# Sorted experts: the expert numbers of a chunk read behind the first product of its last tile, and their table written in two copies

## The chip, the cores and the metric

The program runs on one core of a Trainium2 chip. The metric is the device time of one execution in microseconds (us), as the median over several runs; lower is better. A core has five engines that run side by side, each with its own instruction queue: TensorE (PE, with its weight loads listed as PEld), VectorE (DVE), ScalarE (ACT), GpSimd (POOL) and SyncE (SP, which issues DMAs). Each queue is fed by a sequencer, a small processor that also executes the instructions for registers, branches and some of the waits on semaphores. In the profile the sequencer of TensorE stands as PEldq.

## The reference, cut to what matters

The network has two layers, each with an attention branch and a gated mixture-of-experts branch. The last part of the second layer is the one that this case is about:

```python
xs = x * scores
order = jnp.argsort(topk_ids)
sorted_x = xs[order]
g = _grouped_mm(sorted_x, routed_gate_w, tokens_per_expert)
u = _grouped_mm(sorted_x, routed_up_w, tokens_per_expert)
d = _grouped_mm(jax.nn.silu(g) * u, routed_down_w, tokens_per_expert)
routed_out = d[inv]
...
x = x + s * g
```

There are 8192 tokens of 128 numbers, 32 experts with a hidden size of 256, and each token goes to one expert. `s` is the attention branch, and the last `g` is the silu of shared plus routed output.

## The kernel before, in words

The kernel works in stages with a barrier between them. Stage 3 computes the second layer's attention and the choice of expert, and scatters each token's row (its scaled input, the attention result, the shared result and the residual) into a sorted buffer `srt` in HBM. The buffer has 96 tiles of 128 rows; all rows of a tile belong to one expert. At the end of stage 3 TensorE transposes the count that tells each tile's expert into one PSUM row, and VectorE's `table_rows` writes it as integers into `TE`: row j of `TE` holds eight numbers, the experts of the four tiles of chunk j-1 and then those of the four tiles of chunk j. It does so in three passes over 32 tiles each, through a small integer tile (L1846 to L1856).

Stage 4 (L1970 to L2200) works through the sorted tiles in 24 chunks of four. All of the routed weights lie in SBUF (`WE1`, `big` in the profile), and a product picks its expert's columns by a register. For a tile t the steps are:

- SP loads the chunk's rows (L2005) and, later, its tails with the other branches' values (L2008).
- PE transposes the rows (L2041), ACT copies the result to SBUF (L2100).
- PE makes the first product, gate and up in one, 512 columns wide (`up`, L2036). Here the weights' columns move past the array, and they are addressed by the expert's register.
- ACT applies silu (L2110), DVE multiplies by the up half (L2132).
- PE transposes the hidden rows (L2046), DVE copies them to SBUF (`turned`, L2136).
- PE makes the second product (`down`, L2055), again addressed by the expert's register.
- Once a chunk: DVE adds the tails (L2142), ACT applies the silu (L2104), DVE weighs and finishes (L2147, L2154, L2155), and POOL scatters the four tiles to the output with four indirect DMAs (L2194) behind a small instruction (L2191) that waits for L2155.

On TensorE the tiles are skewed by hand. An iteration for tile t issues `up(t)`, the row transpose of tile t+2, the hidden transposes of tile t-2 and `down(t-3)`, in this order. Before the four iterations of a chunk the function `experts(j)` reads row j of `TE`, eight registers at once; it is the `TENSOR_LOAD` on L2061. The second half of the eight serves the four `up` of this chunk, the first half serves the three `down` of the chunk ahead that are still due, and for its last iteration the chunk uses the same register list for its own tile.

The first two chunks and the last two are written out, and the twenty between them are a loop of ten rounds with two chunks in each (`pe.Fori`, its branch stands on L2087 in the profile). Inside the loop the semaphore values that are waited for are computed from the loop's counter, so a wait is made of a register instruction (`ALU_OP` or `FUSED_REGOPS`) ahead of the instruction that waits.

Of the kernel before, what the change touches and what calls it, by code (L numbers as in the profile page):

```python
# [25 lines left out]
ALU = mybir.AluOpType  # L26
# [3 lines left out]
P = 128  # L30
C = 128
# [12 lines left out]
E1, F1 = 32, 256  # L44
# [4 lines left out]
SORTED_TILES = NT + E1  # L49
IN_FLIGHT = 4  # L50
# [19 lines left out]
def mixed_layers(nc, x, w0, cols, rows, rot, cst, ws, wsd, we0, wd0, w1, we1, out):  # L70
# [10 lines left out]
    with ctx:  # L81
# [19 lines left out]
        WE1 = big[:, :].rearrange("p (e f) -> p e f", e=E1)  # L101
# [61 lines left out]
        ident = CST[:, C_ID:C_ID + P]  # L163
# [48 lines left out]
        pb = [ps[:, n, :] for n in range(8)]  # L212
# [4 lines left out]
        hT = early([P, 2, FC, S])  # L217
# [331 lines left out]
        part = early([E0, CAP, 4])  # L549
# [651 lines left out]
        TE = sb("TE", [1, SORTED_TILES // IN_FLIGHT + 1, 2 * IN_FLIGHT], I32)  # L1201
# [3 lines left out]
        def stage3():  # L1205
# [28 lines left out]
            end_of, new, dg, base, pages = (late([P, E1]) for _ in range(5))  # L1234
            need = sb("mx_need", [P, E1])
            cnt = sb("mx_cnt", [P, HALF])
            ci = [sb(f"mx_ci{m}", [P, E1], I32) for m in range(2)]
# [13 lines left out]
            xT = [attT, ROT[:, :].rearrange("p (g s) -> p g s", g=2)]  # L1251
            zA = [b.rearrange("p g t c -> p (g t) c") for b in (z, att)]
            n_w = E1 * 768 // HALF
            at = [E1 * 768 - 4 * PT * C]
# [15 lines left out]
            pb = [ps[:, n, :] for n in range(8)]  # L1270
# [35 lines left out]
            with nc.Block() as block:  # L1306
# [384 lines left out]
                def _(dve):  # L1691
# [150 lines left out]

                    def table_rows():

                        dve.wait_ge(s["table"], 1)
                        rows = ci[0][0:1, 0:E1].rearrange("p (j k) -> p j k", k=IN_FLIGHT)  # L1846
                        by_chunk = pb[0][0:1, 0:SORTED_TILES].rearrange("p (n j k) -> p n j k", k=IN_FLIGHT, n=SORTED_TILES // E1)
                        for n in range(SORTED_TILES // E1):
                            dve.drain()
                            dve.tensor_copy(rows, by_chunk[:, n, :, :])  # L1850
                            dve.drain()
                            for at, part in ((0, slice(IN_FLIGHT, 2 * IN_FLIGHT)), (1, slice(0, IN_FLIGHT))):
                                j = at + n * E1 // IN_FLIGHT
                                dve.tensor_scalar(TE[:, j:j + E1 // IN_FLIGHT, part], rows, E1 - 1, None, ALU.bitwise_and)
                        dve.memset(TE[:, 0:1, 0:IN_FLIGHT], 0)
                        dve.memset(TE[:, SORTED_TILES // IN_FLIGHT:, IN_FLIGHT:], 0)  # L1856

                    def step(k):
                        i, m, p = k.i, k.m, k.i - 1
# [110 lines left out]
        def stage4():  # L1970

            n_t = IN_FLIGHT
            chunks = SORTED_TILES // n_t
# [12 lines left out]
            def gu(k):  # L1986
                return ps[:, k % 2, :]

            def xTp(k):
                return ps[:, 2 + k % 2, 0:P]  # L1990

            def hTp(k):
                return ps[:, 4 + k % 2, 0:F1]

            def yp(b):
                return ps[:, 6 + b, :]
# [4 lines left out]
            with nc.Block() as block:  # L2001
# [28 lines left out]
                @block.tensor  # L2030
                def _(pe):
                    def up(t, k, e, first):
                        pe.wait_ge(s["xT"], t + 1)
                        if not first:
                            pe.wait_ge(s["h"], t - 1)
                        pe.matmul(gu(k), xT[k % n_t], WE1[:, e, 0:2 * F1], start=True, stop=True).then_inc(s["gu"], 1)  # L2036

                    def row_transpose(k, b, pairs):
                        if k % n_t == 0:
                            pe.wait_ge(row_in[b], 16 * pairs)  # L2040
                        pe.transpose(xTp(k), xt[b][:, k % n_t, :], ident).then_inc(s["xTp"], 1)  # L2041

                    def hidden_transpose(t, k):
                        pe.wait_ge(s["h"], t + 1)
                        for f in range(2):
                            last = pe.transpose(hTp(k)[:, f * P:(f + 1) * P],  # L2046
                                                hb[k % n_t][:, f * P:(f + 1) * P], ident)
                        last.then_inc(s["hTp"], 1)

                    def down(t, k, b, e):  # L2050
                        pe.wait_ge(s["hT"], t + 1)
                        if k % n_t == 0 and (not isinstance(t, int) or t >= 2 * n_t):
                            pe.wait_ge(s["sum"], t // n_t - 1 if isinstance(t, int) else chunk_of[0] - 1)
                        for f in range(2):
                            last = pe.matmul(yp(b)[:, k % n_t * C:(k % n_t + 1) * C], hT[k % n_t][:, f * P:(f + 1) * P],  # L2055
                                             WE1[:, e, 2 * F1 + f * C:2 * F1 + (f + 1) * C],
                                             start=(f == 0), stop=(f == 1))
                        last.then_inc(s["yp"], 1)

                    def experts(j):  # L2060
                        return nc.values_load_multi_w_load_instructions(  # L2061
                            TE[0:1, bass.ds(j, 1), :], engines=[mybir.EngineType.PE], min_val=0, max_val=E1 - 1,
                            skip_runtime_bounds_check_because="the table holds a count of experts, clamped to E1 - 1")[1]
                    chunk_of = [0]

                    def chunk(q, b, e, first=False, final=False):
                        chunk_of[0] = 2 * q + b
                        for k in range(n_t):
                            t = n_t * (2 * q + b) + k
                            up(t, k, e[n_t + k], first and k < 2)  # L2070
                            if not (final and k >= 2):
                                row_transpose(k + 2, b if k < 2 else 1 - b, q + 1 + b)
                            if not (first and k < 2):
                                hidden_transpose(t - 2, k + 2)
                            if not (first and k < 3):
                                down(t - 3, k + 1, b if k == 3 else 1 - b, e[k + 1])

                    def pair(q, first=False, final=False):
                        for b in range(2):
                            f, l = first and b == 0, final and b == 1  # L2080
                            e = experts(2 * q + b)
                            chunk(q, b, e, f, l)

                    for t in range(2):
                        row_transpose(t, 0, 1)
                    pair(0, first=True)
                    with pe.Fori(1, chunks // 2 - 1) as q:  # L2087
                        pair(q)
                    pair(chunks // 2 - 1, final=True)
                    t, e = SORTED_TILES, experts(chunks)  # L2090
                    for k in range(2):
                        hidden_transpose(t - 2 + k, 2 + k)
                        down(t - 3 + k, 1 + k, 1, e[k + 1])
                    down(t - 1, 3, 1, e[3])

                @block.scalar
                def _(act):
# [185 lines left out]
```

## Time and profile before

| | us |
|---|---|
| median of 3 runs | 1386.27 |
| lowest and highest | 1384.61, 1388.18 |
| the profiled execution, device time | 1387.99 |
| the profiled execution, span from first to last instruction | 1385.5 |
| TensorE matmuls busy | 1191.1 (86% of the span) |
| VectorE, ScalarE, GpSimd busy | 989.9, 783.7, 645.9 |
| mean granted TensorE clock | 0.959 of full speed |

The profile comes from one execution. Busy time is the time in which an engine had at least one instruction under way. Instructions that a sequencer runs alone (register, branch and semaphore instructions, and `TENSOR_LOAD`) are not counted as busy. Stage 4 lies between about 1183 us and the end of the span.

### The profile page before, as it was taken

How to read it: one execution, taken by the hardware profiler on the slowest of the kernel's cores; microseconds unless marked ns; L12 is line 12 of the kernel's file. 1: busy time of each engine (PE TensorE's matmuls, PEld its weight loads, DVE VectorE, ACT ScalarE, POOL GpSimd, SP SyncE). 2: the span in 40 equal slices, each digit the busy share in tenths (PEclk: the TensorE clock that was granted, in tenths of full speed). 3: DMA queues.
4: the chain of work that ended last, by engine and by line, in shares of the span. 5: the costliest groups of instructions: out<-in, count | busy, mean ns of one | idle time of the engine just before them, and what ended most of it. 6: DMA issues, size and time to landing. Idle time of an engine off the chain costs nothing. (4 is left out here: it accounts for less than half of the span.)

```text
span 1385.5 us, 28473 instructions
## 1 busy us (share of the span) xinstructions
PE 1191.1 (86%) x7942; PEld 902.7 (65%) x7943; DVE 989.9 (71%) x3562; ACT 783.7 (57%) x1993; POOL 645.9 (47%) x1096
## 2 busy tenths in 40 slices
PE   5999999999972899999999956988888896799993
PEld 3778777777851677767677744766676674456662
DVE  3777777777777777777777636888888886366663
ACT  2575656666630666656565625777777774233331
POOL 3343434343312354545454523556555645056665
PEclk9999999999985999999999977999999999899997
DMA  4424242424301222222222113344344232356651
GB/s 163 144 96 143 88 154 85 150 92 144 127 24 38 51 50 59 44 61 42 61 42 61 35 37 94 113 140 133 120 138 144 91 134 89 119 163 189 184 175 52
DMA packets 140717, 140.83 MB, mean 102 GB/s; under 512 B 18662, under 2 KB 119885, under 8 KB 140672
## 3 DMA queue, kind: packets, MB, share of 16 engines
q1 hardware_dynamic: 125248, 111.38, 25.8%
q0 software_dynamic: 14848, 26.77, 6.9%
q10 hardware_dynamic: 576, 2.15, 0.4%
q8 instruction: 19, 0.31, 0.1%
q14 instruction: 26, 0.21, 0.0%
HBM read 67.63 MB, written 62.13 MB: 94 GB/s over the span
## 5 line engine op out<-in xcount | busy, mean ns | idle before, releaser
L377 ACT ACTIVATE pr<-ps,nmx 128x256 f32<-128x256 f32 x256 | 117.9, 474 | 43.9 <-DVE nmx L424 42.8
L365 ACT ACTIVATE big<-ps,BHS 128x256 f32<-128x256 f32 x256 | 107.1, 470 | 61.3 <-PE ps L242 52.5
L242 PE MATMUL ps<-big,W 128*128 128x256 f32 x512 | 130.9, 400 | 5.6 <-ACT big L370 5.5
L255 PE MATMUL ps<-W,big 128*128 128x128 f32 x1024 | 130.7, 281 | 0.0
L255 PEld LDWEIGHTS ps<-W,big 128*128 128x128 f32 x1024 | 119.6, 192 | 14.0 <-ACT big L365 6.0
L2194 POOL DMA_INDIRECT out<-X,io x96 | 100.5, 1047 | 34.4 <-issue 34.4
L242 PEld LDWEIGHTS ps<-big,W 128*128 128x128 f32 x512 | 95.7, 197 | 26.9 <-ACT big L370 15.7
L2036 PE MATMUL ps<-big,zT 128*128 x192 | 102.5, 616 | 9.6 <-DVE pr L2132 9.1
L424 DVE TENSOR_REDUCE nmx<-ps 128x2 f32<-128x512 f32 x128 | 82.4, 686 | 38.5 <-PE ps L277 21.4
L1003 POOL DMA_INDIRECT ffn<-big,si x64 | 94.0, 1468 | 26.5 <-issue 26.5
L2110 ACT ACTIVATE pr<-ps 128x256 f32<-128x256 f32 x96 | 36.9, 384 | 108.5 <-PE ps L2036 95.4
L432 DVE COPY pT<-ps 128x512 f32<-128x512 f32 x128 | 82.6, 686 | 9.8 <-PE ps L286 9.1
L2132 DVE TENSOR_TENSOR pr<-ps,pr 128x256 f32<-128x256 f32 x96 | 40.7, 424 | 65.7 <-ACT pr L2110 63.3
L510 POOL TENSOR_TENSOR big<-big,EPS 128x2 f32<-128x2 f32 x32 | 6.7, 210 | 155.0 <-DVE big L459 155.0
L277 PE MATMUL ps<-qk 64*128 64x256 f32 x512 | 73.5, 406 | 2.6 <-DVE v L417 2.6
L295 PE MATMUL ps<-pT,v 128*64 128x256 f32 x512 | 69.4, 392 | 3.8 <-DVE pT L432 0.5
L262 PE MATMUL ps<-zT,W 128*128 128x256 f32 x256 | 72.6, 408 | 0.0
L286 PE MATMUL ps<-CST,pr 128*128 128x128 f32 x512 | 68.4, 276 | 1.0 <-ACT pr L377 1.0
L286 PEld LDWEIGHTS ps<-CST,pr 128*128 128x128 f32 x512 | 56.5, 141 | 15.9 <-issue 7.7
L370 ACT ACTIVATE big<-ps,COL 128x256 f32<-128x256 f32 x64 | 36.1, 564 | 53.8 <-PE ps L232 53.8
L415 DVE SCALAR_TENSOR_TENSOR qk<-ps,COL,ROT 128x256 f32<-128x256 f32 x128 | 55.0, 471 | 11.9 <-PE ps L266 9.8
L450 DVE SCALAR_TENSOR_TENSOR big<-ps,rsm,X 128x128 f32<-128x128 f32 x128 | 39.0, 347 | 34.1 <-PE ps L304 25.2
(280 smaller groups left out, 3233.9 us busy)
## 6 DMA issues: line engine op xcount, KB each, us to landing
srt<-big SPq DMA_DIRECT2D x16, 1584.0 KB, 5.7
X<-srt SPq DMA_DIRECT2D x24, 800.0 KB
big<-we SPq DMA_DIRECT2D x16, 768.0 KB, 7.6
big<-we SPq DMA_DIRECT2D x16, 384.0 KB, 3.5
X<-srt SPq DMA_DIRECT2D x24, 256.0 KB
big<-x SPq DMA_DIRECT2D x32, 128.0 KB, 2.2
X<-big SPq DMA_DIRECT2D x32, 128.0 KB, 2.2
xw<-big SPq DMA_DIRECT2D x32, 128.0 KB, 1.9
```

The lines of the kernel that those rows point to most:

```text
L242: last = pe.matmul(pb[2 * g + f // 2][:, f % 2 * S:(f % 2 + 1) * S], W0[:, l, 512 + f * P:512 + (f + 1) * P], zT2[:, g, :], start=True, st ...
L255: last = pe.matmul(pb[4 + g][:, t * C:(t + 1) * C], hT[:, g, f, t * P:(t + 1) * P], W0[:, l, 1024 + f * C:1024 + (f + 1) * C], start=(f == ...
L262: pe.matmul(pb[4 + g][:, j * S:(j + 1) * S], w, zT1[:, g, :], start=True, stop=True)
L277: last = pe.matmul(pb[2 * g + h][:, t * S:(t + 1) * S], qk[d, g, 0, t * P:(t + 1) * P], qk[d, g, 1, :], start=True, stop=True)
L286: last = pe.transpose(pb[2 * g + h][:, k * S + t * P:k * S + (t + 1) * P], pr[:, g, h, t, k * P:(k + 1) * P], ident)
L365: act.activation(hT[:, g, f, :], pb[2 * g + half][:, f % 2 * S:(f % 2 + 1) * S], ACT.Silu, bias=BHS[:, l, f:f + 1], scale=GELU).then_inc(s ...
L377: last = act.activation(pr[:, g, h, t, :], pb[2 * g + h][:, t * S:(t + 1) * S], ACT.Exp, bias=nmx[:, g, h * TPU + t:h * TPU + t + 1], accu ...
L424: last = dve.tensor_reduce(nmx[:, g, h * TPU:(h + 1) * TPU], pb[2 * g + h].rearrange("p (t k) -> p t k", t=TPU), X_AXIS, ALU.max, negate=True)
L432: dve.tensor_copy(pT[:, g, h, :, :].rearrange("p k q -> p (k q)"), pb[2 * g + h])\
L1003: pool.indirect_dma_start(out=ffn0[:, :], out_offset=bass.IndirectOffsetOnAxis(ap=si[:, n:n + 1], axis=0), in_=ye[half, n // 2, :], in_off ...
L2036: pe.matmul(gu(k), xT[k % n_t], WE1[:, e, 0:2 * F1], start=True, stop=True).then_inc(s["gu"], 1)
L2194: pool.indirect_dma_start(out=out[:, :], out_offset=bass.IndirectOffsetOnAxis(ap=io[b][:, k:k + 1], axis=0), in_=ob[b][:, k, :], in_offset ...
```

## The change

In `experts`, nothing changes but what it returns: the eight registers split into `old` (the chunk ahead of the row's) and `new` (the row's own chunk). What changes is where it is called. A chunk on TensorE now begins one instruction group later: `chunk(c)` first reads row c+1 of the table, and then issues the row transpose, hidden transposes and `down` that belong to the iteration of `up(4c+3)`; the three iterations of `up(4c+4)` to `up(4c+6)` follow, and `up(4c+7)` closes it. The order of the matmuls and transposes is the same as before. The read, and in the loop the branch with it, moves from between `down` and the next `up` to between `up` of a chunk's last tile and the row transpose behind it. `down` of chunk c uses `old`, the `up` of chunk c+1 use `new`. A new function `first_chunk` reads row 0 ahead of the first row transposes. `up`, `row_transpose`, `hidden_transpose` and `down` take the same waits as before, in another notation.

In `table_rows` two memsets of the unused corners move ahead of the wait. Then two copies write the whole table from PSUM in the two places, and after a drain one instruction clamps all of `TE`.

```diff
                     def table_rows():
 
+                        n_c = SORTED_TILES // IN_FLIGHT
+                        dve.memset(TE[:, 0:1, 0:IN_FLIGHT], 0)
+                        dve.memset(TE[:, n_c:n_c + 1, IN_FLIGHT:2 * IN_FLIGHT], 0)
                         dve.wait_ge(s["table"], 1)
-                        rows = ci[0][0:1, 0:E1].rearrange("p (j k) -> p j k", k=IN_FLIGHT)
-                        by_chunk = pb[0][0:1, 0:SORTED_TILES].rearrange("p (n j k) -> p n j k", k=IN_FLIGHT, n=SORTED_TILES // E1)
-                        for n in range(SORTED_TILES // E1):
-                            dve.drain()
-                            dve.tensor_copy(rows, by_chunk[:, n, :, :])
-                            dve.drain()
-                            for at, part in ((0, slice(IN_FLIGHT, 2 * IN_FLIGHT)), (1, slice(0, IN_FLIGHT))):
-                                j = at + n * E1 // IN_FLIGHT
-                                dve.tensor_scalar(TE[:, j:j + E1 // IN_FLIGHT, part], rows, E1 - 1, None, ALU.bitwise_and)
-                        dve.memset(TE[:, 0:1, 0:IN_FLIGHT], 0)
-                        dve.memset(TE[:, SORTED_TILES // IN_FLIGHT:, IN_FLIGHT:], 0)
+                        by_chunk = pb[0][0:1, 0:SORTED_TILES].rearrange("p (j k) -> p j k", k=IN_FLIGHT)
+                        dve.tensor_copy(TE[:, 0:n_c, IN_FLIGHT:2 * IN_FLIGHT], by_chunk)
+                        dve.tensor_copy(TE[:, 1:n_c + 1, 0:IN_FLIGHT], by_chunk)
+                        dve.drain()
+                        dve.tensor_scalar(TE[:, :, :], TE[:, :, :], E1 - 1, None, ALU.bitwise_and)
...
-                    def chunk(q, b, e, first=False, final=False):
-                        chunk_of[0] = 2 * q + b
+                        return e[:n_t], e[n_t:]
+
+                    def chunk(c, b, q, last=False):
+
+                        old, new = experts(c + 1)
                         for k in range(n_t):
-                            t = n_t * (2 * q + b) + k
-                            up(t, k, e[n_t + k], first and k < 2)
-                            if not (final and k >= 2):
-                                row_transpose(k + 2, b if k < 2 else 1 - b, q + 1 + b)
-                            if not (first and k < 2):
-                                hidden_transpose(t - 2, k + 2)
-                            if not (first and k < 3):
-                                down(t - 3, k + 1, b if k == 3 else 1 - b, e[k + 1])
-
-                    def pair(q, first=False, final=False):
+                            if k:
+                                up(n_t * (c + 1) + k - 1, k - 1, new, False)
+                            if not (last and k == 3):
+                                row_transpose((k + 1) % n_t, 1 - b if k < 3 else b, q + 1 + b if k < 3 else q + 2)
+                            hidden_transpose(n_t * c + 1 + k, (k + 1) % n_t)
+                            down(c, k, b, old)
+                        up(n_t * (c + 1) + 3, 3, new, False)
+
+                    def first_chunk():
+                        e = experts(0)[1]
+                        for k in range(2):
+                            row_transpose(k, 0, 1)
+                        for k in range(n_t):
+                            up(k, k, e, k < 2)
+                            if k < 3:
+                                row_transpose((k + 2) % n_t, 0 if k < 2 else 1, 1)
+                            if k == 2:
+                                hidden_transpose(0, 0)
+
+                    first_chunk()
+                    chunk(0, 0, 0)
+                    chunk(1, 1, 0)
+                    with pe.Fori(1, chunks // 2 - 1) as q:
                         for b in range(2):
-                            f, l = first and b == 0, final and b == 1
-                            e = experts(2 * q + b)
-                            chunk(q, b, e, f, l)
-
-                    for t in range(2):
-                        row_transpose(t, 0, 1)
-                    pair(0, first=True)
-                    with pe.Fori(1, chunks // 2 - 1) as q:
-                        pair(q)
-                    pair(chunks // 2 - 1, final=True)
-                    t, e = SORTED_TILES, experts(chunks)
-                    for k in range(2):
-                        hidden_transpose(t - 2 + k, 2 + k)
-                        down(t - 3 + k, 1 + k, 1, e[k + 1])
-                    down(t - 1, 3, 1, e[3])
+                            chunk(2 * q + b, b, q)
+                    chunk(chunks - 2, 0, chunks // 2 - 1, last=True)
+                    old = experts(chunks)[0]
+                    for k in range(n_t):
+                        if k < 3:
+                            hidden_transpose(SORTED_TILES - 3 + k, (k + 1) % n_t)
+                        down(chunks - 1, k, 1, old)
```

## Rows read from the trace of the kernel before

**Rows 1.** The page: busy us and share by engine; a DMA issue, us to landing.

```profile
PE 1191.1 (86%) x7942; PEld 902.7 (65%) x7943; DVE 989.9 (71%) x3562; ACT 783.7 (57%) x1993; POOL 645.9 (47%) x1096
...
big<-x SPq DMA_DIRECT2D x32, 128.0 KB, 2.2
```

**Rows 2.** Busy time by windows: PE, PEld, DVE, ACT, POOL, clock, DMA share, GB/s.

```profile
1300.00:1350.00 50.00, 47.38 (x253) 31.32 (x251) 34.66 (x84) 19.03 (x63) 30.85 (x35) 1.00 0.59 178
```

**Rows 3.** Timeline of PE over two chunk starts, the second with the loop's branch.

```profile
1295.09 1.02 PE L2036 MATMUL ps<-big,zT 128*128 x2
...
1297.15 1.12 PE L2036 MATMUL ps<-big,zT 128*128 x2 [0.26 <-DVE pr L2132]
...
1298.88 1.02 PE L2036 MATMUL ps<-big,zT 128*128 x2
...
1302.15 1.02 PE L2036 MATMUL ps<-big,zT 128*128 x2
1303.01 0.27 PE L2041 MATMUL ps<-CST,X 128*128 128x128 f32 x1
...
1303.34 0.61 PE L2055 MATMUL ps<-big,pT 128*128 x4
1304.46 1.12 PE L2036 MATMUL ps<-big,zT 128*128 x2 [0.52 <-DVE pr L2132]
```

**Rows 4.** Waits of PE in stage 4: us in total, times, longest.

```profile
PE ps L2036 <- DVE pr L2132: 9.1, 21, 0.6
```

**Rows 5.** PE's sequencer by source line: duration in ns (min/median/max), first and last start.

```profile
L2061 PEldq TENSOR_LOAD <-TE x25: 588/592/796, 1186.0 to 1360.0; - x25
...
L2061 PEldq TENSOR_LOAD <-TE x2: 589/590/592, 1296.2 to 1303.5; - x2
...
L2055 PEldq FUSED_REGOPS  x2: 46/46/46, 1295.8 to 1296.0; - x2
...
L2055 PEldq FUSED_REGOPS  x2: 46/46/46, 1302.8 to 1302.9; - x2
...
L2036 PEldq FUSED_REGOPS  x1: 46/46/46, 1301.7 to 1301.7; - x1
...
L2087 PEldq COMPARE_BRANCH  x10: 76/208/238, 1214.7 to 1346.4; - x10
```

**Rows 6.** Timeline of PE: `up(4)` and `up(94)`.

```profile
1194.51 1.12 PE L2036 MATMUL ps<-big,zT 128*128 x2 [0.44 <-DVE pr L2132]
...
1357.52 1.02 PE L2036 MATMUL ps<-big,zT 128*128 x2
```

**Rows 7.** Timeline of ACT and PE at the late silu of one chunk.

```profile
1236.17 0.39 ACT L2110 ACTIVATE pr<-ps 128x256 f32<-128x256 f32 x1 [1.83 <-PE ps L2036]
...
1237.58 0.71 PE L2055 MATMUL ps<-big,pT 128*128 x4 [0.23 <-DVE pT L2136]
```

**Rows 8.** Timeline of DVE around the same chunk starts.

```profile
1298.72 0.42 DVE L2132 TENSOR_TENSOR pr<-ps,pr 128x256 f32<-128x256 f32 x1 [0.74 <-ACT pr L2110]
...
1302.33 0.41 DVE L2136 COPY pT<-ps 128x256 f32<-128x256 f32 x1
...
...
1304.47 0.68 DVE L2142 TENSOR_TENSOR X<-ps,X 128x512 f32<-128x512 f32 x1
```

**Rows 9.** Timeline of POOL: a chunk in the loop, and the last three chunks.

```profile
1303.84 0.19 POOL L2191 TENSOR_TENSOR carrier<-carrier 128x1 f32<-128x1 f32 x1 [1.28 <-DVE X L2155]
...
1360.84 0.19 POOL L2191 TENSOR_TENSOR carrier<-carrier 128x1 f32<-128x1 f32 x1 [1.19 <-DVE X L2155]
...
1366.42 0.21 POOL L2191 TENSOR_TENSOR carrier<-carrier 128x1 f32<-128x1 f32 x1
...
1372.16 0.21 POOL L2191 TENSOR_TENSOR carrier<-carrier 128x1 f32<-128x1 f32 x1
```

**Rows 10.** Timeline at the end of stage 3: the table, and the barrier.

```profile
1174.27 0.18 DVE L1850 CAST mx_ci<-ps 1x32 int32<-1x32 f32 x1 [0.24 <-issue]
...
1182.88 0.10 POOL L2198 MEMSET carrier<- 128x4 f32 x1 [5.55 <-POOLq L1306]
```

More of the change, by code:

```diff
@@ L2035, in up @@
                             pe.wait_ge(s["h"], t - 1)
-                        pe.matmul(gu(k), xT[k % n_t], WE1[:, e, 0:2 * F1], start=True, stop=True).then_inc(s["gu"], 1)
+                        pe.matmul(gu(k), xT[k], WE1[:, e[k], 0:2 * F1], start=True, stop=True).then_inc(s["gu"], 1)
                     def row_transpose(k, b, pairs):
-                        if k % n_t == 0:
+                        if k == 0:
                             pe.wait_ge(row_in[b], 16 * pairs)
-                        pe.transpose(xTp(k), xt[b][:, k % n_t, :], ident).then_inc(s["xTp"], 1)
+                        pe.transpose(xTp(k), xt[b][:, k, :], ident).then_inc(s["xTp"], 1)
                     def hidden_transpose(t, k):
@@ L2045, in hidden_transpose, with down @@
                         for f in range(2):
-                            last = pe.transpose(hTp(k)[:, f * P:(f + 1) * P],
-                                                hb[k % n_t][:, f * P:(f + 1) * P], ident)
+                            last = pe.transpose(hTp(k)[:, f * P:(f + 1) * P], hb[k][:, f * P:(f + 1) * P], ident)
                         last.then_inc(s["hTp"], 1)
[L2050 to L2053, printed above, removed]
+                    def down(c, k, b, e):
+                        pe.wait_ge(s["hT"], n_t * c + k + 1)
+                        if k == 0 and (not isinstance(c, int) or c >= 2):
+                            pe.wait_ge(s["sum"], c - 1)
                         for f in range(2):
-                            last = pe.matmul(yp(b)[:, k % n_t * C:(k % n_t + 1) * C], hT[k % n_t][:, f * P:(f + 1) * P],
-                                             WE1[:, e, 2 * F1 + f * C:2 * F1 + (f + 1) * C],
+                            last = pe.matmul(yp(b)[:, k * C:(k + 1) * C], hT[k][:, f * P:(f + 1) * P],
+                                             WE1[:, e[k], 2 * F1 + f * C:2 * F1 + (f + 1) * C],
                                              start=(f == 0), stop=(f == 1))
@@ L2060, in experts @@
                     def experts(j):
-                        return nc.values_load_multi_w_load_instructions(
+                        e = nc.values_load_multi_w_load_instructions(
                             TE[0:1, bass.ds(j, 1), :], engines=[mybir.EngineType.PE], min_val=0, max_val=E1 - 1,
                             skip_runtime_bounds_check_because="the table holds a count of experts, clamped to E1 - 1")[1]
-                    chunk_of = [0]
-                    def chunk(q, b, e, first=False, final=False):
-                        chunk_of[0] = 2 * q + b
+                        return e[:n_t], e[n_t:]
```

## The prediction

> **What bounds the kernel now.** The page came first: matmuls keep TensorE busy for 86% of the span, ahead of every other engine [rows 1]. The change touches only the last stage (about 1183 us to the end), so I read that stage by windows: in 50 us of its steady part TensorE is busy 47.4 us, DVE 34.7, POOL 30.9, ACT 19.0, and the clock is granted in full [rows 2]. What is left to win there is TensorE's idle time and little else.
>
> The timeline shows where it lies. From 1298.88 to 1302.15 two tiles pass in 3.27 us, 1.635 us each, with no gap. At the start of a chunk the step from one `up` to the next is 2.06 us (1295.09 to 1297.15), and 2.31 us where the loop's branch lies in it (1302.15 to 1304.46). The step behind is 1.73 us instead of 1.635, because the first weight load of an `up` that finds the array empty is not hidden [rows 3]. A chunk start thus costs 0.52 us (3.79 less 3.27), and one with the branch 0.68 + 0.10 = 0.78 us.
>
> The table of waits puts these gaps down to DVE's product (L2132) [rows 4]. The reader should distrust it: the product that `up(t)` waits for is that of tile t-2, two steps older. The sequencer tells what really came last. It finishes the addresses of the last `down` at 1296.0, starts the `TENSOR_LOAD` at 1296.2, and that takes 0.59 us; in the loop the same goes 1302.9, then the branch, 1303.5 and again 0.59 us [rows 5]. The load ends at 1296.8 and 1304.1; `up` follows at 1297.15 and 1304.46 [rows 3], 0.35 us later both times, which is the address and wait arithmetic ahead of it. So the gap is the sequencer's: it can't issue `up` before it has read the expert. The same rows show that the load does not need an empty array: it starts at 1303.5 while the four products of `down` run from 1303.34 to 1303.95.
>
> Over the stage: from `up(4)` at 1194.51 to `up(94)` at 1357.52 lie 163.0 us [rows 6]. Ninety steps at 1.635 are 147.15, so 15.9 us are excess over 22 chunk starts. Ten with the branch at 0.78 and twelve without at 0.52 make 14.0. The other 1.9 belong mostly to three chunk starts where a silu came about 0.7 us late for a reason that I can't see: one stands at 1236.17, and made `down` wait 0.23 us at 1237.58 [rows 7]. There the load, which stands behind `down`, came late too.
>
> **The change, part by part.** *The read moves behind `up(4c+3)`.* TensorE's order of work stays; only load and branch move. The question is whether they now fit in time that the array spends on that `up`. From the loop's second chunk: the addresses of `up(4c+3)` are done at 1301.75, while it starts in the array at 1302.15, and the next work, the row transpose, is due at 1303.01, 0.86 us on [rows 3, 5]. Without the branch the load begins 0.2 us behind the last addresses, as now (1296.0 to 1296.2), and ends at 1301.75 + 0.2 + 0.6 = 1302.55, 0.45 us early. With the branch the distance is 0.6 us (1302.9 to 1303.5), and it ends at 1302.95: 0.06 us early. The weights of this transpose are then loaded late, which costs something between nothing and 0.3 us (the 0.10 us of an unhidden weight load, and up to 0.2 of issue). I take 0.1 us, the row of the unhidden load.
>
> Next in the queue behind the load are the hidden transposes, whose wait has long been met, and `down(4c)`, which waits for DVE's copy. That copy ends at 1302.74 (1302.33 + 0.41) [rows 8], and its addresses are made at 1302.8 [rows 5]. So the sequencer stands idle until 1302.8 anyway: without the branch the load is free, with it `down` is issued some 0.2 us later than now, and the following `up` at about 1303.6 instead of 1303.4, against 1303.78 when the array is due for it. This is the point with the least slack, but it is slack.
>
> By the Trainium skill (Advanced Engine Details and Errata, Sequencer Loop) further engine instructions can be read and queued while a control instruction executes. By that the transposes would not wait for the load at all, and the 1.0 us that I charge below for ten branches would be nothing; no row shows it, because the `up` behind the load today needs its register.
>
> *Removed, summed to `up(94)`.* 15.9 us of excess. At the start `up(4)` found the array idle for 0.44 us and had 0.10 us of open weight load [rows 6]: 0.5. The first read overlaps the wait for the first rows (today it starts at 1186.0 and takes 0.80 us [rows 5]): 0.1. Together 16.5. *Kept:* ten branches at 0.1 are 1.0; three late silus at the 0.23 that `down` waits by itself are 0.7; twelve other chunk starts at 0.03 are 0.4. Together 2.1. The saving is **14.4 us**.
>
> *Does it reach the end?* The span ends on POOL: chunk 22's stores begin at 1366.42 and chunk 23's at 1372.16 with no idle time before them. But chunk 21's begin at 1360.84 after 1.19 us of waiting for DVE, which waited for `up(94)` [rows 9]. So everything up to 1360.84 moves with TensorE, and the 25 us behind it stay as they are. The last read (at 1360.0 today) lies ahead of work that only these POOL-bound stores wait for: nothing.
>
> *What could now bind.* The chunk's pitch is 7.06 us without the branch and 7.31 with it (2.06 or 2.31, 1.73 and twice 1.635), and falls to about 6.6. POOL needs 5.74 us for a chunk with no wait (1366.42 to 1372.16), and waits 1.28 us of each today: some 0.6 stay [rows 9]. DVE's product behind a chunk start has 0.74 us of idle time at 1298.72; less 0.52 that leaves 0.2. With the branch: DVE's sum ends at 1305.15 (1304.47 + 0.68) [rows 8]; the product started 1.57 us behind its `up` (1297.15 to 1298.72), 1.47 with the weight load hidden, so it is due at 1303.88 + 1.47 = 1305.35, and again 0.2 us stay. DMA engines are busy 0.59 of the time [rows 2], and would be 0.65.
>
> *The table.* The three passes begin at 1174.27 and the next stage only at 1182.88, when POOL's wait for the scattered rows is over (5.55 us of idle time) [rows 10]. DVE's part is over before 1177. Saving a microsecond of it is worth nothing; it would have to grow by six to be seen.
>
> Against its own time the profiled execution goes from 1387.99 to 1373.6. It stood 1.7 us above the median of the runs, to which I apply the same saving: 1386.27 - 14.4 = **1371.9, say 1372 us**.
>
> **Rivals.** (1) *The read is hidden, as above:* 1372; 0.72, own range 1369.5 to 1375. (2) *Another engine takes the gap.* DVE's product has 0.2 us of slack and POOL 0.6. If under the tighter pitch one of them comes late by 0.3 us at each of 22 chunk starts, 6.6 us come back: 1378.5. For it: the late silus already use up more than 0.2; against: none of the two is late today. 0.12. (3) *The sequencer is late after all,* because the register work that I took from today's order grows or the weight load wants more lead: 0.4 with each of ten branches above my 0.1 and 0.2 at twelve others, 6.4 us: 1378.3. Against it: the load ends 0.45 us early without the branch. 0.09. (4) *Nothing moves,* because POOL's stores set the stage's pace: the 1.28 us waits speak against it. 1386; 0.03. (5) *Slower: instruction fetch at the loop's branch.* The ten branches of today take 76 to 238 ns [rows 5], so the loop's start was always at hand. The rewritten queue lies elsewhere in memory, and if each of nine backward branches had to fetch its target, the nearest price is a small load from HBM, 2.2 us to landing [rows 1]: 9 x 2.2 = 20 us, against 14.4 saved, about 1392. It decides from 1.6 us a branch on. 0.04.
>
> The Trainium skill (Runtime: NRT & Kernel Launch, Instruction fetch mechanics) says that a taken branch whose target is outside the fetched window stalls for a fetch; by today's branch rows no such stall is there.
>
> **How the numbers follow.** Cases 1 to 3 give 1369.5 (all excess gone, 16.5 us, and no cost kept) to 1378.5, and hold 0.93. The range is 1369 to 1378.5: it leaves out cases 4 and 5 and the far edges of 2 and 3, less than 2 in 10. Within 0.3% (4.2 us) is about what a measurement of this kernel can't tell from no change. Cases 1 to 3 are faster by 7.8 us or more: 0.93; same 0.03; slower 0.04.
>
> **What would show it.** In the changed kernel's trace the `TENSOR_LOAD` should start while `up` runs, the step between two `up` should be 1.64 us at chunk starts without the branch and up to 1.75 with it, and the 9.1 us of PE's wait at L2036 should fall below 1. POOL's waits should shrink to about 0.6 us a chunk, and the last 25 us should be unchanged. I am wrong if `up` steps of over 1.9 us remain at each branch (case 3), if PE's waits on DVE's copy or product appear instead (case 2), or if the branches take microseconds (case 5).

## The result and the profile after

The changed kernel ran at 1380.6 us (median of 11 runs, 1378.86 to 1383.55), the kernel before beside it at 1387.32 us (11 runs, 1384.61 to 1389.41). The ratio is 0.9954, with a 95% interval of 0.9946 to 0.9961: faster, but by 6.7 us and not by 14.4, and above the forecast range. The profiled execution took 1381.36 us with a span of 1379.5.

The timeline of TensorE has the two ends of the stretch that the sum was made over (start, duration, engine and line, operation):

```profile
1194.94 1.02 PE L2033 MATMUL ps<-big,zT 128*128 x2
...
1351.45 1.02 PE L2033 MATMUL ps<-big,zT 128*128 x2
```

From `up(4)` to `up(94)` lie 156.51 us, where there were 163.0 [rows 6]. Less the 147.15 of ninety undisturbed steps, the excess is 9.4 us instead of 15.9, and the forecast had kept only 2.1. So the missing time lies inside this stretch, not in the tail. Does the reading of the experts still cost it? TensorE's sequencer by source line, over the run and at one chunk start, and the array's timeline at that start:

```profile
L2058 PEldq TENSOR_LOAD <-TE x25: 587/592/778, 1184.8 to 1352.6; - x25
L2089 PEldq COMPARE_BRANCH  x10: 76/208/215, 1219.3 to 1346.0; - x10
...
L2058 PEldq TENSOR_LOAD <-TE x1: 594/594/594, 1283.0 to 1283.0; - x1
```

```profile
1281.62 1.02 PE L2033 MATMUL ps<-big,zT 128*128 x2
...
1283.26 1.02 PE L2033 MATMUL ps<-big,zT 128*128 x2
1284.12 0.27 PE L2038 MATMUL ps<-CST,X 128*128 128x128 f32 x1
...
1284.89 1.02 PE L2033 MATMUL ps<-big,zT 128*128 x2
```

No. The load of 0.59 us lies at 1283.0 to 1283.6, before and while `up` (1283.26) runs, and both steps around it are 1.63 to 1.64 us. The branch takes what it took [rows 5]. In the table of waits the 9.1 us at `up` [rows 4] are gone, and another row has grown:

```profile
PE ps L2052 <- DVE pT L2139: 4.6, 11, 0.7
...
PE ps L2033 <- ACT zT L2103: 0.2, 1, 0.2
```

TensorE now waits in `down` (L2052) for VectorE's copy of the hidden rows (L2139): 4.6 us in 11 places up to 1352 us. Before it was 0.4 us in 2 places in the same part of the stage, and a third wait of 0.8 lay behind `up(94)`. By windows the stage is not full either (the columns are those of [rows 2]):

```profile
1300.00:1350.00 50.00, 48.16 (x257) 32.06 (x258) 35.53 (x87) 20.06 (x66) 29.30 (x36) 1.00 0.57 171
```

One such place, in the timeline of all engines:

```profile
1274.27 1.02 PE L2033 MATMUL ps<-big,zT 128*128 x2
...
1274.70 0.14 PEld L2038 LDWEIGHTS ps<-CST,X 128*128 128x128 f32 x1 [0.24 <-issue]
...
1275.24 0.38 PE L2043 MATMUL ps<-CST,pr 128*128 128x128 f32 x2
1275.25 1.06 POOL L2197 DMA_INDIRECT out<-X,io  x1 [0.30 <-issue]
...
1275.66 0.38 ACT L2113 ACTIVATE pr<-ps 128x256 f32<-128x256 f32 x1 [1.42 <-PE ps L2033]
...
1276.08 0.43 DVE L2135 TENSOR_TENSOR pr<-ps,pr 128x256 f32<-128x256 f32 x1 [0.62 <-issue]
1276.60 0.14 PEld L2038 LDWEIGHTS ps<-CST,X 128*128 128x128 f32 x1 [0.51 <-issue]
...
1277.14 0.42 DVE L2139 COPY pT<-ps 128x256 f32<-128x256 f32 x1 [0.63 <-PE ps L2043]
...
1277.81 0.71 PE L2052 MATMUL ps<-big,pT 128*128 x4 [0.56 <-DVE pT L2139]
...
1278.36 1.02 PE L2033 MATMUL ps<-big,zT 128*128 x2
```

The hidden transposes end at 1275.62. DVE's copy of them starts at 1277.14 and gives TensorE as the releaser, 1.5 us later, although DVE is free from 1276.51. The silu of the `up` of 1274.27 starts 1.39 us behind it, where an undisturbed one starts 1.06 us behind (1270.67 to 1271.73 in the trace of chip 12 below). Then `down` waits 0.56 us, and the step to the `up` at 1278.36 is 2.46 us (from 1275.90). The array never stopped up to this wait of `down`: it had gone on to later products while the news of the earlier ones was still out. The recorded semaphore events agree. None of TensorE's four semaphores shows an update between 1275.68 and 1277.12, nor between 1268.48 and 1270.66, and the `down` that ended at 1269.13 is told at 1270.66, 1.5 us late. VectorE's updates in these stretches come at once (1269.24 and 1276.52), and ScalarE's silu of 1275.66 releases VectorE's product at 1276.08. I call these held updates.

Two limits belong to that. The profile models the ends of matmuls, so it can't tell whether the last write to PSUM or only the update came late. And the records of updates have gaps of their own: this trace holds 93 or 94 of 96 for each of TensorE's semaphores, but 76 to 81 for four of VectorE's and ScalarE's. One of TensorE's is missing in the second stretch, where VectorE's copy began in time at 1269.15. So the late starts of the consumers are the evidence, and the records only support it.

In this trace 27 silus of tiles 5 to 93 start more than 0.1 us later than 1.06 behind their `up`, 14.0 us in sum, 1.14 at most; in the trace before there are 12, 3.6 us in sum, 0.74 at most. Of the excess of 9.4 us, 9.1 lie in twenty steps over 1.7 us.

The tail is as forecast. POOL's timeline at the last three chunks (chunk 21 to 23):

```profile
1354.77 0.19 POOL L2194 TENSOR_TENSOR carrier<-carrier 128x1 f32<-128x1 f32 x1 [1.16 <-DVE X L2158]
1360.57 0.23 POOL L2194 TENSOR_TENSOR carrier<-carrier 128x1 f32<-128x1 f32 x1
```

Chunk 21's stores still wait for DVE, chunk 22's don't, and from the first to the end lie 24.7 us, as before [rows 9].

### The profile page after: what moved, and what is told of

It reads as the page before. It is cut to its first block and busy times, and to the rows that moved or that the text cites. A ratio compares the mean times of both kernels' runs of the same rounds, so it can differ in the third digit from the quotient of the medians.

```text
span 1379.5 us, 28492 instructions
## 1 busy us (share of the span) xinstructions
PE 1190.0 (86%) x7942; PEld 903.0 (65%) x7943; DVE 988.8 (72%) x3556; ACT 785.3 (57%) x1993; POOL 640.6 (46%) x1096
## 5 line engine op out<-in xcount | busy, mean ns | idle before, releaser
L242 PE MATMUL ps<-big,W 128*128 128x256 f32 x512 | 127.9, 394 | 5.6 <-ACT big L370 5.5
L2197 POOL DMA_INDIRECT out<-X,io x96 | 95.5, 995 | 34.4 <-issue 34.4
L2052 PE MATMUL ps<-big,pT 128*128 x384 | 60.7, 281 | 5.3 <-DVE pT L2139 5.2
```

The lines of the kernel that those rows point to most:

```text
L242: last = pe.matmul(pb[2 * g + f // 2][:, f % 2 * S:(f % 2 + 1) * S], W0[:, l, 512 + f * P:512 + (f + 1) * P], zT2[:, g, :], start=True, st ...
L2197: pool.indirect_dma_start(out=out[:, :], out_offset=bass.IndirectOffsetOnAxis(ap=io[b][:, k:k + 1], axis=0), in_=ob[b][:, k, :], in_offset ...
```

## The experiments

The runs were given to five chips, which the results number 6, 3, 15, 12 and 7; the first result doesn't name its chip. "Late" counts the silus of tiles 5 to 93 as above. "Excess" is the time from `up(4)` to `up(94)` less 147.15 us, always from the profiled execution.

### Reads and scatters, chip 6

Without the reads, in both orders (all chunks use the experts of the first read, so the products are those of other experts):

```diff
+                    kept = []
                     def experts(j):
+                        if not kept:
+                            kept.append(read(j))
+                        return kept[0]
+                    def read(j):
```

> The changed kernel with its table read once, at the start; all 25 other reads are left out, so every tile uses the experts of the first four. Measured by the time from up(4) to up(94) less 147.15 us, the excess: 15.9 us before, 9.4 us in the changed kernel. Theory H (the semaphore updates of TensorE are held back while the chunk's rows are loaded and its last scatter is written, and that takes what the read gave back): the read is already free, so the excess stays at 8 to 9.5 us and the time within 1.5 us of the changed kernel's. Rival Q (TensorE's sequencer is still late at the chunk starts, because of the read): the excess falls to 3 us or less and the time by about 6 us.

> The kernel before with its table read once, at the start; the other reads are left out in the same way. Theory H: what the change gave is what taking the read out gives, because the held updates are then exposed in the same way: the excess falls from 15.9 to between 8 and 11 us and the time by 5 to 8 us. Rival Q: the read is worth its full 0.6 us at each of 22 chunk starts, so the excess falls by 13 us, to 3.

Without the scatters, in both orders (only the last two chunks are stored, and DVE doesn't wait for stores):

```diff
-                            dve.wait_ge(put[b], 16 * n_t * q)
...
-                        for k in range(n_t):
+                        for k in range(n_t) if isinstance(j, int) else ():
                             pool.indirect_dma_start(out=out[:, :],
...
-                    with pool.Fori(0, chunks // 2) as q:
+                    with pool.Fori(0, chunks // 2 - 1) as q:
```

> The changed kernel without the scatter of the first 22 chunks to the output (those rows of the output are not written); the last two chunks are stored. Theory H with the scatter as its source: the silus come on time and the excess is 3 us or less. Rival Q: the excess stays at 9 us, since nothing in TensorE's queue changes. Rival D (the row load alone holds the updates back): the excess stays at 6 us or more, with silus late behind each row load.

> The kernel before without the scatter of the first 22 chunks, as a control. Theory H: only the part of the excess that came from late silus goes, 1.5 to 2.5 us, and about 14 us stay, because the read still stands in the open; with the changed kernel without its scatter, the difference is then the 12 to 14 us that were forecast for the change. Rival Q: the two differ by 6 to 7 us, as with the scatter.

| | us (runs) | ratio, 95% | excess | late silus |
|---|---|---|---|---|
| changed, no reads | 1383.43 (10) | 0.9965, 0.9953 to 0.9978 | 11.15 | 29 |
| before, no reads | 1380.1 (5) | 0.9939, 0.9917 to 0.9961 | 8.87 | 28 |
| changed, no scatters | 1363.12 (1) | | 1.22 | 0 |
| before, no scatters | 1379.99 (1) | | 13.74 | 0 |

The kernel before ran at 1388.32 here (14 runs). ScalarE's silus in the timeline, the changed kernel without reads:

```profile
1241.29 0.38 ACT L2120 ACTIVATE pr<-ps 128x256 f32<-128x256 f32 x1 [1.08 <-PE ps L2033]
1243.97 0.38 ACT L2120 ACTIVATE pr<-ps 128x256 f32<-128x256 f32 x1 [2.13 <-PE ps L2033]
1244.56 0.38 ACT L2120 ACTIVATE pr<-ps 128x256 f32<-128x256 f32 x1
1246.80 0.38 ACT L2120 ACTIVATE pr<-ps 128x256 f32<-128x256 f32 x1 [0.40 <-PE ps L2033]
```

and without scatters:

```profile
1241.83 0.38 ACT L2113 ACTIVATE pr<-ps 128x256 f32<-128x256 f32 x1 [0.56 <-PE ps L2033]
1243.46 0.38 ACT L2113 ACTIVATE pr<-ps 128x256 f32<-128x256 f32 x1 [1.08 <-PE ps L2033]
1245.10 0.38 ACT L2113 ACTIVATE pr<-ps 128x256 f32<-128x256 f32 x1 [1.08 <-PE ps L2033]
```

Where nothing is held, a silu follows the last by 1.63 to 1.64 us. With the updates held one comes after 2.68 us and the next 0.59 behind it: two updates arrived close together. Three things follow. The reads are not the cause: without them the updates are held all the same. With the scatters gone no silu is late in either order. And then the change is worth 13.74 - 1.22 = 12.5 us of excess. The whole times of the two orders without scatters are not to be set beside the others: the end of the stage is shorter too (19.8 us from `up(94)` to the end in the changed order, against 28.2 in the changed order without reads). What the experiment takes out is more than the transfers, POOL's work for them and VectorE's wait for their landing as well, so which of these matters is open.

The experiment also shows why the kernel before hides the fault. It has the chunk-start gap and, in its own trace, 12 late silus, 3.6 us in sum. With the reads taken out, and that gap with them, the old order has 28, 19.5 us in sum, and reaches only 1380.1, near the 1380.6 of the changed kernel in the first result (the changed kernel itself didn't run on chip 6).

Both runs without scatters came out as theory H had them. Without reads, the old order's excess of 8.87 did, and its time fell by 8.2 us where 5 to 8 were expected. The changed order missed on both: 11.15 where 8 to 9.5 were expected, and a time 2.8 us over the changed kernel's. That it is also 3.3 us slower than the old order without reads isn't explained.

### The row load, and the table, chips 3 and 15

In the first trace the holds that I looked at began in the row load of the next chunk (the load issued at 1273.96 was moving its packets from 1275.0 to 1276.9), so I suspected its meeting with the scatters. I call that theory H1. One tile later (and two, by `+ 2`), in both orders:

```diff
-                                sp.wait_ge(s["xTp"], n_t * j + n_t)
+                                sp.wait_ge(s["xTp"], n_t * j + n_t + 1)
```

> The changed kernel, complete, with the row load of chunk j+2 issued one tile later: SP waits for one more row transpose, so the transfer begins about 1.6 us later and falls behind the last scatter of a chunk instead of ahead of it. Theory H1 (the last scatter lands late because the row load's small packets stand ahead of it in the DMA engines, and the held updates end with it): the silus come nearly on time, the excess falls from 9.4 to between 1.5 and 5 us, and the time to 1373 to 1377 us. Rival H2 (the row load holds the updates wherever it stands): the late silus move to another tile, and the excess stays at 7 us or more.

> The kernel before, complete, with the row load one tile later, as in a_laterows. If the two act together as theory H1 has it (the late silus of before are few, because its chunk starts leave room), only 1.5 to 2.5 us go: excess 13.5 to 14.5, time 1383 to 1385 us, and the change on top of it is worth about 12.5 us. If the row load's place were worth as much by itself as on top of the change (8 us), the time would be 1377 us.

> The changed kernel, complete, with the row load two tiles later. Theory H1: the row load falls past the last scatter as well and nothing is held: excess 1 to 2 us like one tile later, as long as the rows still arrive in time for their transpose. Rival: the one tile was a lucky place, and here silus are late again, excess 5 us or more.

Coarser packets (one run of four tiles for each partition, so the rows are other rows), a quarter of the rows (three of four tiles work on old rows), a quarter of the tails (three of four tiles of tails, with their output positions, are old ones), and two scatters of four (half of the tiles aren't stored):

```diff
+                        n = n_t if isinstance(j, int) else 1
+                        sp.dma_start(xt[b][:, 0:n, :], srt_t[:, bass.ds(n_t * j, n), 0:C]).then_inc(row_in[b], 16)
...
-                        for k in range(n_t):
+                        for k in range(n_t // 2):
```

> The changed kernel with the same bytes in a row load, but read as one piece of 2048 bytes for each partition instead of four of 512 (the rows are wrong then). Theory H1: the count of packets matters little as long as the bytes stand ahead of the scatter: excess 6 to 9 us. Rival H3 (the number of small packets holds the updates): a quarter of the packets, excess 4 us or less.

> The changed kernel with only the first of a chunk's four row tiles loaded in the loop (the others keep old rows). Theory H1: a quarter of the packets stands ahead of the scatter, which lands about 1 us sooner: excess 2 to 5 us. A rival in which the scatter alone holds the updates, whatever stands ahead of it: the excess stays at 8 to 9 us.

> The changed kernel with only the first of a chunk's four tail tiles loaded in the loop (the others keep old tails). The tails are the largest transfer, 0.8 of 1.06 MB a chunk. Theory H1: the first scatters land sooner, but the row load still stands ahead of the last one, and the excess stays at 6 us or more. Rival H4 (it is the load on the DMA engines as a whole): excess 3 us or less.

> The changed kernel, with the row load in its own place, but only the first two of a chunk's four scatters (half of the output's rows are not written). Theory H1: the last scatter of a chunk is issued before the row load, nothing is held behind it, excess 1 to 3 us. Rival: the row load holds the updates as soon as any scatter is about, excess 6 us or more.

And the changed order with the three passes of the kernel before that write the table:

> The changed kernel with the old three passes of table_rows. Both theories: the same as the changed kernel within 1.5 us, since the barrier behind the table waits for POOL's scatter. If the table's part carried some of the 6.7 us, the time would be 1382 us or more.

| | chip | us (runs) | ratio, 95% | excess | late |
|---|---|---|---|---|---|
| changed, rows 1 tile later | 3 | 1372.2 (5) | 0.9902, 0.9884 to 0.992 | 1.25 | 0 |
| changed, coarse rows | 3 | 1372.26 (1) | | 1.77 | 0 |
| changed, a quarter of the rows | 3 | 1372.67 (1) | | 1.23 | 0 |
| changed, a quarter of the tails | 3 | 1371.54 (1) | | 1.80 | 0 |
| before, rows 1 tile later | 15 | 1386.36 (10) | 1.0, 0.9989 to 1.0011 | 13.78 | 0 |
| changed, rows 2 tiles later | 15 | 1370.06 (1) | | 1.27 | 0 |
| changed, two scatters | 15 | 1361.4 (1) | | 1.21 | 0 |
| changed, old table | 15 | 1371.72 (4) | 0.9897, 0.9881 to 0.9914 | 1.66 | 0 |

The kernel before ran at 1385.33 on chip 3 and at 1386.45 on chip 15. Read alone, the first row looked like a cure: 1372.2 us. But coarse rows gave the same, and then the last row came, which differs from the changed kernel only in how the table is written, far ahead of stage 4, and that too ran at 1371.7 with no silu late. Seven edits of the changed kernel and one of the kernel before, none with a late silu, don't say that any of them cured the fault. What all eight lacked was the unedited kernel on the same chip. Several also missed what theory H1 expected: an excess of 6 to 9 us for coarse rows, 6 or more for a quarter of the tails, 2 to 5 for a quarter of the rows and 1.5 to 5 for rows one tile later, and 1383 to 1385 us for the kernel before with late rows. The old table was to run like the changed kernel of the first result. Two scatters and rows two tiles later (1 to 3 and 1 to 2 us) came out as expected, but so they would have without any fault to cure. The 1361.4 us of two scatters hold a shorter end of the stage, as without scatters.

### The unedited kernel once more, chips 12 and 7

> The changed kernel, unedited, once more: it has not yet run beside the versions that run at about 1371 us. Theory H (TensorE's semaphore updates are held back where the chunk's row load meets the four scatters, whatever the chip and the run): 1379 to 1382 us, an excess of 8 to 11 us over 90 steps of 1.635, 20 or more silus late. Rival R (whether the updates are held back is a matter of the chip or of the run, not of the program, and the load's place and size were never the cause): if this chip is one where they are not held, 1370 to 1374 us, an excess of 1 to 2 us and no late silu.

> The changed kernel with the chunk's row load one tile later, once more. Theory H: 1370 to 1374 us with an excess of 1 to 2 us, 7 to 10 us under the unedited changed kernel in the same job. Rival R: within 2 us of the unedited changed kernel, be that at 1371 or at 1380 us.

> The changed kernel with the old three passes that write the table, once more, beside the unedited changed kernel. Theory H, in which the table has no part: within 2 us of the unedited changed kernel, at 1379 to 1382 us. Rival R: within 2 us of it as well, but at 1370 to 1374 us. Rival T (the new writing of the table is what brings the held updates): 1370 to 1374 us here, with the unedited changed kernel at 1379 to 1382.

> The changed kernel, unedited, a third time, for the chip that this job is given. In the job before it ran at 1372.5 us with no late silu, against 1380.6 us at first. Theory C (whether TensorE's semaphore updates are held back depends on the chip or the run): either near 1372 us with an excess of 1 to 2 us, the kernel before at about 1386, or near 1380 us with an excess of 8 to 11 us, the kernel before at about 1388. Rival P (the first result was a matter of those runs alone and belongs to no chip): near 1372 us.

> The changed kernel with the chunk's row load one tile later, beside the unedited one. Where the updates are held for the unedited kernel: 1371 to 1374 us if the meeting of the row load with the scatters is what holds them, 1378 to 1383 us if the scatters alone do. Where they are not held for the unedited kernel: within 1 us of it, and nothing is learnt of the load.

> The changed kernel with one of the four tiles of a chunk loaded in the loop (the other three products work on old rows). Where the updates are held for the unedited kernel: an excess of 1 to 3 us and at most five late silus if the load's packets hold them, 8 to 11 us and over 20 late silus if the scatters alone do. Where they are not held: 1370 to 1374 us, and nothing is learnt of the load.

| | chip | us (runs) | ratio, 95% | excess | late |
|---|---|---|---|---|---|
| changed, unedited | 12 | 1372.48 (5) | 0.9906, 0.9887 to 0.9925 | 1.65 | 0 |
| rows 1 tile later | 12 | 1371.41 (4) | 0.9897, 0.9877 to 0.9917 | 1.24 | 0 |
| old table | 12 | 1372.28 (4) | 0.9904, 0.9883 to 0.9926 | 1.41 | 0 |
| changed, unedited | 7 | 1371.83 (4) | 0.9895, 0.9879 to 0.9912 | 1.57 | 0 |
| rows 1 tile later | 7 | 1371.5 (4) | 0.9894, 0.9877 to 0.991 | 1.25 | 0 |
| a quarter of the rows | 7 | 1373.61 (1) | | 1.20 | 0 |

The kernel before ran at 1385.77 and 1385.6. So the unedited kernel runs at the forecast 1372 here, 13.3 and 13.8 us ahead of before, and no edit moves it. What the edits seemed to gain on chips 3 and 15 is thus no evidence for the row load, nor for the table. Nor do these chips refute them, since nothing is held there. All six came out as expected for chips without held updates, and where held updates were expected for the unedited kernel, that missed.

The traces carry a mark that parts the two kinds of execution before stage 4 begins. Up to 1183 us, those of `before`, the first result and the four versions on chip 6, with or without scatters, hold 6970 to 7011 recorded updates of the DMA queues' semaphores. The fourteen traces of chips 3, 15, 12 and 7 hold 7579 to 7584. So the two versions without scatters did run in the condition in which updates are held elsewhere, and had no late silu all the same; and the first result was not a matter of its own runs alone. What the missing records come from isn't known.

The profile of the unedited kernel on chip 12, first by a window of 50 us, then TensorE's waits in stage 4:

```profile
1290.00:1340.00 50.00, 50.00 (x276) 33.64 (x275) 36.86 (x91) 20.49 (x69) 30.93 (x38) 1.00 0.62 192
```

```profile
PE ps L2052 <- DVE pT L2139: 0.6, 1, 0.6
PE ps L2033 <- ACT zT L2103: 0.2, 1, 0.2
```

and the timeline over a chunk start with the loop's branch, and the sequencer's rows for it:

```profile
1270.67 1.02 PE L2033 MATMUL ps<-big,zT 128*128 x2
...
1271.73 0.38 ACT L2113 ACTIVATE pr<-ps 128x256 f32<-128x256 f32 x1 [1.08 <-PE ps L2033]
...
1272.30 1.02 PE L2033 MATMUL ps<-big,zT 128*128 x2
1273.16 0.27 PE L2038 MATMUL ps<-CST,X 128*128 128x128 f32 x1
...
1273.61 0.71 PE L2052 MATMUL ps<-big,pT 128*128 x4
1274.15 1.02 PE L2033 MATMUL ps<-big,zT 128*128 x2
```

```profile
L2089 PEldq COMPARE_BRANCH  x1: 208/208/208, 1272.0 to 1272.0; - x1
...
L2058 PEldq TENSOR_LOAD <-TE x1: 673/673/673, 1272.4 to 1272.4; - x1
```

The array is busy for the whole 50 us. The step with the branch is 1.85 us (1272.30 to 1274.15), the one ahead 1.63. The load ends at 1273.1, hardly before the row transpose at 1273.16; it took 0.67 us here, where the prediction counted 0.59. From `up(4)` (1194.75) to `up(94)` (1343.55) lie 148.8 us.

## Why the prediction was right and wrong

**The read is hidden: right, everywhere.** The load runs under `up`, steps without the branch are 1.64 us, `up` no longer waits, and the branch rows are unchanged, which rules out case 5 (instruction fetch). This holds in the first trace too.

**Ten branches at 0.1 us: right, somewhat small.** On chip 12 the nine steps behind a branch from `up(20)` on are 1.76 to 1.85 us, 0.13 to 0.22 over; on chip 6 without scatters 0.12. The rule of the Trainium skill that was weighed there (Advanced Engine Details and Errata, Sequencer Loop: further instructions can be read and queued while a control instruction executes) is not seen at work in the timeline of the result. There the transpose's weight load starts at 1276.60, after 0.51 us of idle time instead of the usual 0.24, just when the read is over:

```profile
L2058 PEldq TENSOR_LOAD <-TE x1: 592/592/592, 1276.0 to 1276.0; - x1
```

**The tail and the table: right.** The last 24.7 us are unchanged, and the old table costs nothing measurable (1372.28 against 1372.48).

**The 1372 of chips 12 and 7: in part luck.** The sum counted 14.4 us off 1386.27. Measured are 13.3 off 1385.77 and 13.8 off 1385.6, and 0.9 and 0.6 us of these lie outside the span from first to last instruction, about which the prediction said nothing: the device time is 2.8 and 2.5 us longer than the span in the kernel before, 1.9 in the changed one (medians). Inside the stretch the undisturbed change takes 13.78 - 1.65 = 12.1 us of excess, where the sum took 13.8, because its 15.9 held 2.1 us of held updates that the old order doesn't show on chip 15. The low edge of case 1 is also a slip: 1386.27 less 16.5 is 1369.8, not 1369.5, which moves nothing.

**The step that failed** is a term of the kept costs, "three late silus at the 0.23 that `down` waits by itself are 0.7". I had seen the silu come late "for a reason that I can't see" and carried over what it had cost there: 0.23 us in each of three places. Price and count both grew. In the kernel before the fault shows in just three steps, those to `up(20)`, `up(28)` and `up(52)`, with 2.64, 2.82 and 2.73 us where the same order without held updates has 2.04 to 2.08. (At the first it is VectorE's copy that comes late; ten further silus are 0.15 to 0.25 late and cost nothing.) In the changed kernel fifteen steps of 1.79 to 2.57 us carry it, and `down` waits 0.42 us on average in eleven places. TensorE's pause at each chunk start, which the change removes, had kept most updates clear of the holds. That the pause did so is inferred from the counts: 12 late silus with it, 27 to 29 without it, in either order. In the changed kernel the fault costs 9.36 - 1.65 = 7.7 us of excess, with 27 late silus where 12 had been. In the kernel before it cost 15.86 - 13.78 = 2.1 us (the 13.78 is that of rows one tile later on chip 15; 13.74 without scatters). The difference, 5.6 us, is most of what separates the 13.3 and 13.8 us saved on chips 12 and 7 from the 6.7 saved at first; the rest isn't assigned. Rival 2 had the right form (VectorE has 0.2 us of slack, something comes late by about 0.3 us at each chunk start, 6.6 us come back), but what came late was news, not an engine's work. It was given 0.12 and kept out of the range beyond its own 1378.5.

**What is shown and what isn't.** Shown on chip 6: the lateness stays without the reads and goes away with the scatters, the latter by one profiled execution in each order. Shown by the unedited kernel on chips 12 and 7: the same program runs without the lateness, 8 to 9 us faster. Whether it belongs to the chip or to the hour of the job isn't known, since no chip was given twice. Nor is it known, where updates are held, whether the row load has a part beside the scatters: all versions that would tell ran where none were held. The beginning of the holds in the row load is an observation of timing, nothing more. Why TensorE's updates are held stays open.

## What to carry to other kernels

A gap that a change removes may be what hides lateness from elsewhere. Adding up the lateness seen today is not a safe bound either: here the 12 late silus were late by 3.6 us in sum, and the fault then cost 7.7, because the gap had kept most of the late starts from showing at all. An unexplained late start in a trace is a term with an unknown cost and an unknown count, and the range has to leave room for one at every place that the change tightens. And every set of experiments needs the unedited changed kernel beside it on the same chip: eight versions seemed free of a fault by their edits, on chips whose traces show no sign of it at all.

## What the runs showed of the hardware

News of TensorE's finished work reached the other engines up to 1.5 us late (transposes that ended at 1275.62, told at 1277.12) while the array and VectorE's updates went on, in a stage that keeps the DMA engines some 57% busy with loads and scatters. ScalarE's silus started up to 1.14 us late in the changed kernel, one 2.24 in the old order without reads. The same program on other chips showed none of it, with nearly the same DMA share (0.62) and the granted clock at 1.00 in both windows. A busy share of TensorE of 48.2 us in 50 against 50.0 in 50 was the whole difference in the window rows, and the kernel before showed the matter in its median by only about 2 us (1387.3 and 1388.3 against 1385.3 to 1386.5).
